# Attention layer 0: values as their own fills, heavy fills one to three slots, three score banks and two for transposed probabilities

## The reference

```python
x = x + attn0(layernorm(x))
q, k, v = (n @ W.T + n @ Bm.T @ A.T * 2.0 for each of q, k, v)   # 16 heads of 16
s = q @ k.T / 4 + slopes[h] * (i - j) + causal mask
o = softmax(s) @ v
attn0 = o @ Wp.T
```

## Time and profile before

| | |
|---|---|
| Median of three runs | 2434.92 us (2432.59 to 2435.51) |
| Profiled execution, its own time | 2434.53 us |
| its span, first to last instruction | 2432.7 us |
| TensorE products busy | 2027.4 us, 83% |
| TensorE weight loads busy | 1435.8 us, 59% |
| VectorE busy | 1743.7 us, 72% |
| ScalarE busy | 1465.2 us, 60% |
| GpSimd busy | 1033.4 us, 42% |
| mean granted clock | 0.938 |
| row maxima of layer 0's attention, first to last | 56.0 to 690.7 us |
| layer 0's last projection taken | 708.1 us |

### The profile page before, as it was taken

The page is one execution under the profiler, slowest core; times in us unless marked ns, Lnnn a source line. Parts: engine busy times, 40 slices in busy tenths (PEclk is TensorE's granted clock), DMA queues, the critical chain, the costliest instruction groups (busy, mean ns, idle before and its releaser), DMA issues. The chain is left out here.

```text
span 2432.7 us, 56283 instructions
## 1 busy us (share of the span) xinstructions
PE 2027.4 (83%) x18118; PEld 1435.8 (59%) x18119; DVE 1743.7 (72%) x3667; ACT 1465.2 (60%) x2894; POOL 1033.4 (42%) x1226
## 2 busy tenths in 40 slices
PE   3988888888873699568699999989898999739999
PEld 2665565566663366336476767666676767625665
DVE  3776777677767244449679696968787787589997
ACT  1766666666655244348568686877778687534443
POOL 4524252434203100188856474655656475032222
PEclk8999999999975799779899999999999999959999
DMA  6000000000004323101200000000000000000000
GB/s 229 1 2 1 1 0 1 1 1 0 1 28 171 93 87 92 40 9 21 33 2 2 3 2 2 2 3 2 3 2 3 2 2 2 27 10 11 17 17 24
DMA packets 53133, 57.79 MB, mean 24 GB/s; under 512 B 7120, under 2 KB 47216, under 8 KB 52896
## 3 DMA queue, kind: packets, MB, share of 16 engines
q1 hardware_dynamic: 46240, 45.00, 5.9%
q0 software_dynamic: 6656, 9.85, 1.9%
HBM read 36.22 MB, written 18.61 MB: 23 GB/s over the span
## 5 line engine op out<-in xcount | busy, mean ns | idle before, releaser
L1019 ACT ACTIVATE prob_sb<-a_bank,neg_max_sb 128x128 f32<-128x128 f32 (+3 forms) x512 | 255.4, 528 | 196.9 <-DVE neg_max_sb L1092 193.7
L1092 DVE TENSOR_REDUCE neg_max_sb<-a_bank 128x1 f32<-128x128 f32 (+3 forms) x512 | 236.6, 486 | 177.1 <-PE a_bank L894 162.8
L371 PE MATMUL a_bank<-w_in_sb,xnT_sb 128*128 128x512 f16 x1152 | 289.9, 390 | 29.2 <-DVE t_buf_sb L579 20.8
L531 DVE TENSOR_REDUCE neg_max_sb<-a_bank 128x1 f32<-128x128 f32 (+3 forms) x512 | 235.7, 481 | 98.8 <-PE a_bank L288 98.0
L434 ACT ACTIVATE prob_sb<-a_bank,neg_max_sb 128x128 f32<-128x128 f32 (+3 forms) x512 | 258.8, 536 | 58.9 <-DVE neg_max_sb L531 54.6
L442 ACT ACTIVATE p_hi_sb<-a_bank 128x384 f16<-128x384 f32 (+1 forms) x384 | 204.0, 531 | 111.3 <-PE a_bank L297 110.3
L538 DVE TENSOR_TENSOR p_lo_sb<-a_bank,p_hi_sb 128x384 f16<-128x384 f32 (+1 forms) x384 | 227.6, 594 | 52.8 <-ACT p_hi_sb L442 50.6
L453 ACT ACTIVATE stack_sb<-a_bank 128x1024 f16<-128x1024 f16 (+1 forms) x256 | 209.5, 819 | 33.4 <-PE a_bank L342 31.5
L907 PE MATMUL a_bank<-ident_f_sb,prob_sb 128*128 128x128 f32 x1280 | 208.8, 279 | 4.1 <-DVE probT_sb L1100 2.3
L297 PE MATMUL a_bank<-ident_f_sb,prob_sb 128*128 128x128 f32 x1280 | 207.2, 277 | 0.6 <-ACT prob_sb L434 0.6
L707 POOL TENSOR_TENSOR rope_w_sb<-t_buf_sb,sin_sb 128x256 f32<-128x256 f32 x128 | 124.8, 975 | 169.8 <-DVE t_buf_sb L579 167.9
(11 more groups left out here) (251 smaller groups left out, 5494.0 us busy)
## 6 DMA issues: line engine op xcount, KB each, us to landing
sorted_rows<-zeros_sb SPq DMA_DIRECT2D x1, 4992.0 KB, 22.0
x_in_sb<-sorted_rows SPq DMA_DIRECT2D x39, 128.0 KB, 2.1
sorted_results<-y_moe_sb SPq DMA_DIRECT2D x39, 128.0 KB, 1.7
x_sb_sb<-L_attn_x SPq DMA_DIRECT2D x8, 512.0 KB, 10.6
w_raw_sb<-L_ffn_gate_bank SPq DMA_DIRECT2D x8, 512.0 KB, 4.2
w_raw_sb<-L_ffn_up_bank SPq DMA_DIRECT2D x8, 512.0 KB, 5.0
w_raw_sb<-L_ffn_down_bank SPq DMA_DIRECT2D x8, 512.0 KB, 6.1
out<-x_sb_sb SPq DMA_DIRECT2D x32, 128.0 KB, 1.7
```

What stands on the lines that cost most here:

```text
L371: last = pe.matmul(out, xnT[:, x, c, j * P:(j + 1) * P], w["in"][:, w_, c, cols], start=k == 0, stop=k == len(terms) - 1)
L531: last = dve.tensor_reduce(neg_max[:, i:i + 1], S[(3 * h + g) % 2][:, off:off + L], AX.X, ALU.max, negate=True)
L1019: last = act.activation(prob[g][:, h % 2, off:off + L], S[(3 * h + g) % 2][:, off:off + L], ACT.Exp, bias=neg_max[:, i:i + 1])
L1092: last = dve.tensor_reduce(neg_max[:, i:i + 1], S[(3 * h + g) % 2][:, off:off + L], AX.X, ALU.max, negate=True)
```

## The change

`AT0` gets a seventh list, `AT_V`, and other slots; `LAG_PV` goes from 8 to 14. Of the eight PSUM banks three hold scores (group g always in bank g) and two hold transposed probabilities in turn. A piece computes 256 columns (queries and keys); values are a fill of their own, one per token tile, 256 columns for all 16 heads in two runs of 128 out of `w["in"]`, copied by ScalarE in the slot of the fill. The output products of a batch wait for all four (`s_v`). On VectorE the evacuation of transposed probabilities comes first in the slot. The diff, with hunks that only rename a bank cut:

```diff
-LAGS0 = (4, 1, 8)
-AT0 = ((8, 11, 13, 15), (20, 22, 25, 26), (31, 34, 36, 39), 20, 22, (61, 62, 64, 65))
+LAGS0 = (4, 1, 14)
+AT0 = ((1, 4, 7, 10), (13, 16, 19, 22), (23, 24, 26, 27), (31, 34, 37, 40), 26, 29, (68, 73, 76, 77))
...
-    AT_1, AT_XT, AT_0, AT_OT, AT_YT, AT_PROJ = at
+    AT_1, AT_V, AT_XT, AT_0, AT_OT, AT_YT, AT_PROJ = at
...
-    S, PT, W, ob = banks[0:2], banks[2:5], banks[5:7], banks[7]
+    S, PT, W, ob = banks[0:3], banks[3:5], banks[5:7], banks[7]
...
         out += [("piece", 0, 1, p) for p, at_ in enumerate(AT_1) if at_ == k]
+        out += [("values", 0, j) for j, at_ in enumerate(AT_V) if at_ == k]
...
-    FILLS_W = HEADS + 2 * PIECES + QT + QUADS + CHUNKS + QT
+    FILLS_W = HEADS + 2 * PIECES + QT + QT + QUADS + CHUNKS + QT
...
         def scores(b, h, g):
-            wait(pe, s_exp, G - 1)
+            wait(pe, s_exp, G - 2)
...
-                out = S[(3 * h + g) % 2][:, off:off + L]
+                out = S[g][:, off:off + L]
...
         def transpose_probs(b, h, r):
             if r == 0:
                 wait(pe, s_exp, 3 * (H + 1))
-                wait(pe, s_pta, H)
+            if r < 2:
+                wait(pe, s_ptv, 2 * H - 1 + r)
             else:
-                wait(pe, s_ptv, 2 * H - 2 + r)
+                wait(pe, s_pta, H + 1)
...
-                last = pe.transpose(PT[r][:, n * P:(n + 1) * P],
+                last = pe.transpose(PT[(3 * h + r) % 2][:, n * P:(n + 1) * P],
...
         def pv(b, c, part):
-                wait(pe, s_taken, b * 2 * PIECES + (c // 2 + 1) * PIECES)
+                wait(pe, s_v, (b + 1) * QT)
...
             elif kind == "piece":
-                    last = pe.matmul(out[:, 0:384], xnT[:, c, j * P:(j + 1) * P], w["in"][:, c, half * 384:half * 384 + 384],
+                    last = pe.matmul(out[:, 0:256], xnT[:, c, j * P:(j + 1) * P], w["in"][:, c, half * 384:half * 384 + 256],
...
+            elif kind == "values":
+                j, = a
+                for c in range(C):
+                    last = pe.matmul(out[:, 0:256].rearrange("p (f n) -> p f n", f=2), xnT[:, c, j * P:(j + 1) * P],
+                                     w["in"][:, c, :].rearrange("p (f n) -> p f n", f=2)[:, :, 256:384],
+                                     start=c == 0, stop=c == C - 1)
+                taken[bank] = (s_v, QT, off, j + 1)
...
@@ ScalarE, take @@
+            elif kind == "values":
+                j, = a
+                wait(act, s_fill, n)
+                wait(act, s_pv, b * QUADS)
+                act.activation(v_stage[:, :, j, :, 0:DH], W[bank][:, 0:256].rearrange("p (f h d) -> p f h d", f=2, d=DH),
+                               ACT.Copy).then_inc(s_v, 1)
...
@@ VectorE, take, piece @@
-                                  parts[:, p % 2, :, 0, :], ALU.subtract)
-                wait(dve, s_pv, (b - 1) * QUADS + 2 * half + 2)
-                dve.tensor_copy(v_stage[:, half, p, :, 0:DH],
-                                W[bank][:, 256:384].rearrange("p (h d) -> p h d", d=DH)).then_inc(s_taken, 1)
+                                  parts[:, p % 2, :, 0, :], ALU.subtract).then_inc(s_taken, 1)
...
@@ VectorE, slot @@
+            h, r = divmod(k - LAG_T - LAG_EV, 3)
+            if r and 0 <= h < HEADS:
+                take_probs(b, h, r)
             if k < GROUPS:
                 row_max(b, k // 3, k % 3)
...
-            h, r = divmod(k - LAG_T - LAG_EV, 3)
-            if r and 0 <= h < HEADS:
-                take_probs(b, h, r)
```

More of the change, by code:

```diff
@@ L813, in attention0 @@
     s_taken = sem("piece_taken")
+    s_v = sem("values_ready")
     s_xn = sem("xn_ready")
@@ L1018, in exp @@
                 L = (i + 1) * P
-                last = act.activation(prob[g][:, h % 2, off:off + L], S[(3 * h + g) % 2][:, off:off + L], ACT.Exp, bias=neg_max[:, i:i + 1])
+                last = act.activation(prob[g][:, h % 2, off:off + L], S[g][:, off:off + L], ACT.Exp, bias=neg_max[:, i:i + 1])
                 off += L
@@ L1026, in take_probs @@
             wait(act, s_pv, b * QUADS + h // 4 - 1)
-            act.activation(probT[:, (h // 4) % 2, h % 4, T_AT[0]:T_AT[1]], PT[0][:, :], ACT.Copy).then_inc(s_pta, 1)
+            act.activation(probT[:, (h // 4) % 2, h % 4, T_AT[0]:T_AT[1]], PT[h % 2][:, :], ACT.Copy).then_inc(s_pta, 1)
         def take_out(b, c):
@@ L1091, in row_max @@
                 L = (i + 1) * P
-                last = dve.tensor_reduce(neg_max[:, i:i + 1], S[(3 * h + g) % 2][:, off:off + L], AX.X, ALU.max, negate=True)
+                last = dve.tensor_reduce(neg_max[:, i:i + 1], S[g][:, off:off + L], AX.X, ALU.max, negate=True)
                 off += L
@@ L1100, in take_probs @@
             dve.tensor_copy(probT[:, (h // 4) % 2, h % 4, T_AT[r]:T_AT[r + 1]],
-                            PT[r][:, 0:T_AT[r + 1] - T_AT[r]]).then_inc(s_ptv, 1)
+                            PT[(3 * h + r) % 2][:, 0:T_AT[r + 1] - T_AT[r]]).then_inc(s_ptv, 1)
         def take(kind, b, *a):
```

## The result

The changed kernel takes 2404.06 us (median of four, 2402.13 to 2405.28), the kernel before 2434.02 in the same comparison (2432.59 to 2435.51): ratio 0.9876, 95% interval 0.9859 to 0.9893. That is 30 us off where 20 were forecast. The profiled span is 2402.2 us.

A forecast was written before the change was run, and what follows sets the result against it. No engine is full; TensorE's waits in layer-0 attention bound it. Six steady batches at -2.9 give -17.4, batch 0 -1.0, batch 7 -2.0, start -1.0, tail +1.4: -20.0, from 2434.5 to 2414.5 us; range 2378 to 2441.

The forecast's parts named there:

- more than that: Rival: even loading removes nearly all waits in a layer-0 batch, 5.9 us each, 2393 down to 2380; chance 0.26.
- Knot: Slots 23 to 29, where ten fills meet: TensorE waits of 1.2, 0.8 and 0.6 us for work banks, taken as 2.5.
- Work banks: TensorE's waits for the two work banks fall from 4.3 to 2.5 us per batch: 1.8 saved.
- chain of 3.3: Middle slots: transposes, fill, scores, maximum, exponential and four handovers take 3.3 us, under 4 to 5 per head, so not binding.
- Score banks: Third score bank: of 2.0 us of TensorE's waits for exponentials per batch, 1.3 saved.
- ring: Two banks for transposed probabilities: transposes wait for evacuations, 0.5 us lost per batch; as rival (slower) 2453, chance 0.13.
- Own values: Values as own fills: TensorE even, VectorE relieved of eight copies, ScalarE given four; 0.3 us saved per batch.
- Spreading: Heavy fills one to three slots apart: heaviest two heads 10.0 us instead of 12.0, work bank waits 1.8 less per batch.
- The loop's return: One 2.3 us TensorE wait per batch, counted among those for ScalarE's exponentials; claimed to stay.
- Batch 0: Layer 0's first batch, 71.1 us, has no projections to untangle: 1.0 us saved.
- Tail: Layer 0's end: third quad's output product falls there, two halves of 1.21 less 0.91 idle; 1.4 us lost.
- Weight loads at the value fills: 189 ns loads at the new fills stay covered, cost taken as 0; if all show, 3.0 us per batch.

The follow-up runs named there:

- e5: Kernel after with TensorE's layer-1 loop given head_slot 0 (loop number thought to set code place), nothing else: 2389.71 us, ratio 0.9829 to the kernel before.
- e6: Kernel after with TensorE's layer-1 loop given head_slot 128, nothing else: 2388.2 us, ratio 0.9815 to the kernel before.
- e1: Kernel before with VectorE's layer-0 loop given head_slot 0, nothing else: 2424.94 us, ratio 0.9967.
- e4: Kernel before plus own value fills, new slots and lag 14, old banks and VectorE order, VectorE's layer-0 loop at head_slot 0: 2403.63 us, ratio 0.9874.
- e2: Kernel after with VectorE's layer-0 loop given head_slot 208, nothing else: 2405.25 us, ratio 0.9879 to the kernel before.

## Why the prediction came out as it did

The sign was right and the size was off: 20 forecast, 30 measured, out of larger terms that partly cancel. That 2404 lies in the forecast's 2400 to 2428 is partly luck: without the loss in layer 1, which the prediction excluded, it is 2388 to 2390 (e5, e6), and that is the ground of the rival *more than that*.

- *Start*, -1.0: measured -1.0.
- *Knot*, 1.2, 0.8 and 0.6 us: 1.1, 0.8 and 0.9. Work banks saved 0.9 instead of 1.8: the knot took 2.8 for 2.5, and small waits of 0.6 beside it weren't counted. The handover of 0.2 in that sum stands in no row; in the trace of before a row maximum or an exponential that waited starts 0.04 after the end of what it waited for, and a row maximum 0.20 after the start of TensorE's next record (344.07 to 344.27). With 0.2 the chain of 3.3 would be 3.8 as well; neither decides anything.
- *Score banks* -1.3 and *ring* +0.5: the score waits moved as said (2.0 to 0.7), while the transposes' 0.5 were there before, so the ring cost nothing that shows. But as a term of the batch they were mis-sized: all bank edits with VectorE's order are -1.93 alone and +0.25 on top of the fills. I priced each edit against the waits of before as if these were shared out among the edits; the same slack was there to be won once.
- *Own values* -0.3: +1.37 alone. The stall of ScalarE at a copy whose fill TensorE hasn't computed wasn't in the price, only the copy's 0.374. *Spreading* -1.8: -5.4 against that kernel. The rival *more than that* named -5.9 per batch by evened load; without the return it is -3.8, so two thirds of that rival came true. The objection to it, that ScalarE is in order and busy, had the right engine and the wrong sign: the new slots took idle time off it.
- *The loop's return, "which stays"*: the step that failed first. It was no wait for an exponential in the end but VectorE standing at its return (3.2 to 3.4 us with 26 packets of instructions, 0.22 to 0.24 with 4 in e1), and the row for it was in reach: the wait named ScalarE, ScalarE waited for VectorE, and VectorE's row at 373.19 had idle time put down to issue. It was worth 2.2 us per batch (e1), more than any other single term but the slots.
- *Batch 0* -1.0: -4.4. It was priced by the projections that it lacks; the pieces' share, which it has, is what the slots move (73.9 with values in the old slots, 64.9 in e4). *Batch 7* -2.0: -5.6, by the same as it seems.
- *Tail* +1.4: -1.9, from 17.4 us to 15.5. That is the clock: before, the tail ran at 0.71, after at 1.00. In e1, with the same instructions as before, it ran at 1.00 and took 13.4. Like against like the change adds 2.1, so the sign was right and the term a little small.
- *"The stages behind it keep their instructions, so only this stage's length can move the total"*: the second step that failed, +15.3 us. They keep their instructions but not their time: TensorE's layer-0 loop body ahead of them went from 1399 to 1415 records, and layer 1's seven batches from 917.7 to 933.0 us; with slot 0 or 128 for TensorE's layer-1 loop they take 918.3 and 918.4 (e5, e6).
- *Weight loads at the value fills*: a value fill takes 0.87 (293.75 to the next scores' start at 294.62), as long as the projection fill of 256 columns in the earlier trace rows, so nothing of the loads shows, as assumed:

```profile
293.75 1.03 PE L965 MATMUL a_bank<-w_in_sb,xnT_sb 128*128 128x256 f32 x4
294.62 0.38 PE L895 MATMUL a_bank<-stack_sb 102*128 102x512 bf16 x1
```

With the place of the code out of it (e5 against e1, whose layer 1 are alike), the change is worth some 35 us, -3.9 per steady batch (79.62 to 75.76) against the -2.9 forecast.

## What to carry to other kernels

Before a stall at a loop's return is called fixed, follow it to the engine whose idle time is put down to issue and count the instruction packets of one pass; try the loop's head at another place before tuning around it, and after every edit check the loops behind it, which no diff shows (here 15.3 us). Where an engine takes results in order in the slot in which they are computed, place the computation so that the engine arrives late at them: the stall to look for is on that engine, not on TensorE (here a reading of four kernels, not a run of its own). Edits that draw on the same slack are to be priced as one sum; once the slots were evened, the banks brought nothing.

## What the runs showed of the hardware

The same loop of 329 records on VectorE returns in 0.22 to 0.24 us at slot 0 (e1) and in 3.2 to 3.4 without a number (before). TensorE's loop of 2805 records costs 15 us over seven batches as it stands in the kernel after (933.0) and nothing visible at slots 0 and 128 (918.3 and 918.4); the amount fetched doesn't tell them apart: 85 packets of 16 KiB over layer 1's batches both before and after, 81 in e5 and 86 in e6. Without a number its batches took 922.1 us with a layer-0 loop of 1383 TensorE records, 917.7 with 1399, 933.0 with 1415, 935.2 with 1431 and 933.4 with 1434. The mean clock over these batches is 0.98 in the kernels at 916 to 922 us and 0.97 in those at 933 to 935.

The granted clock showed the stall in layer 0 too. Batch 2 of the kernel before took 82.46 us at 0.98, between batches at 1.00:

```profile
208.90:291.37 82.47, 71.92 (x624) 49.85 (x624) 58.80 (x141) 52.91 (x106) 30.77 (x64) 0.98 0.00 0
```

In after, e2 and e4, whose returns are short or covered, all steady batches read 1.00; in e1 all but the first, with 0.98. In before the clock is at 0.50 to 0.51 for 3.4 us right behind the first, third and fifth return (210.4 to 213.8, 374.3 to 377.7 and 538.1 to 541.5), and reads 1.00 behind the second and fourth, whose gaps are as long. So a gap of this length goes with the drop and doesn't always bring it; it wasn't tested by itself.
